# Two more steps of an attention loop turned by way of DRAM and VectorE

## The reference

```python
x = _layernorm(x + attn(x, Wq, Wk, Wv, Wg, Ws, Wo, g_norm_weight))    # 16 heads, DK 64, M 64, DV 128
x = _layernorm(x + xattn(x, ctx, xWq, bq, xWk, bk))
x = _layernorm(x + ffn(x, w_gate, w_up, w_down))
...
# attn, for each head and token t (p = exp(s - z), g the decay, z = cumlogsumexp(s)):
hk = hk * g[:, None, :] + k[..., None] * p[:, None, :];  ok = q @ hk
pv = softmax(ok)
hv = hv * g[..., None] + p[..., None] * v;               ov = pv @ hv
o  = rmsnorm(ov) * g_norm_weight * silu(x @ Wg);         y  = o @ Wo
# xattn: attention = softmax(query key^T) of ctx; x_m = x @ attention
# ffn: activations of 8 bits, ternary weights, Hadamard transform before w_down
```

## Time and profile before

| | before |
|---|---|
| median of 3 runs | 1484.67 us (1484.51 to 1484.93) |
| time of the profiled execution | 1485.11 us |
| its span, first to last instruction | 1483.3 us |
| TensorE busy | 1448.3 us (98%) |
| VectorE busy | 1091.2 us (74%) |
| ScalarE, GpSimd busy | 637.7 us (43%), 435.9 us (29%) |
| mean granted TensorE clock | 0.998 |
| DMA traffic | 166.53 MB, 112 GB/s in the mean |

### The profile page before, as it was taken

How to read it: one execution, slowest core, us unless ns; L and a number is a source line. 1 busy time by engine, 2 the same in 40 slices (tenths; PEclk the granted TensorE clock), 3 DMA queues, 4 the chain that set the end, 5 groups by cost and what they waited for, 6 DMA issues and landing times.

```text
span 1483.3 us, 23970 instructions
## 1 busy us (share of the span) xinstructions
PE 1448.3 (98%) x9240; PEld 1167.8 (79%) x9240; DVE 1091.2 (74%) x2062; ACT 637.7 (43%) x1205; POOL 435.9 (29%) x283
## 2 busy tenths in 40 slices
PE   8999999999999999999999999999999999999998
PEld 6888888888888888888888888878888646666675
DVE  5567766666667777777677687688787886977788
ACT  4333333333324333333333334234343466776775
POOL 0311011211205445435554423221421343333320
PEclk9999999999999999999999999999999999999999
DMA  4554433443524444435555311101211225444452
GB/s 158 176 138 128 120 97 104 124 119 94 152 71 136 118 139 132 132 110 130 163 157 165 118 44 51 51 8 36 78 44 35 88 79 184 122 129 144 154 172 92
DMA packets 213297, 166.53 MB, mean 112 GB/s; under 512 B 89664, under 2 KB 174528, under 8 KB 213184
## 3 DMA queue, kind: packets, MB, share of 16 engines
q1 hardware_dynamic: 191920, 133.27, 30.4%
q10 hardware_dynamic: 21264, 31.73, 7.2%
HBM read 115.02 MB, written 49.94 MB: 111 GB/s over the span
## 4 chain that ended last, share of the span: by engine, by line
PE 85%; DVE 7%; DMA 2%; POOL 2%; ACT 2%; issue 1%; SPq 0%; POOLq 0%; ACTq 0%; DVEq 0%
PE bank L490 17%; PE bank L496 17%; PE bank L493 17%; PE bank L723 6%; PE bank L618 4%; PE bank L738 4%; PE bank L759 3%; PE bank L580 2%; PE bank L553 2%; PE bank L604 2%; DVE AM L1198 1%; PE bank L575 1%; PE bank L561 1%; PE bank L588 1%; DVE OKM L1176 1%
## 5 line engine op out<-in xcount | busy, mean ns | idle before, releaser
L490 PE MATMUL bank<-Wh,X 128*128 128x512 f32 x512 | 205.6, 402 | 0.1
L496 PE MATMUL bank<-Wh,X 128*128 128x512 f32 x512 | 200.0, 391 | 0.0
L493 PE MATMUL bank<-Wl,X 128*128 128x512 f32 x512 | 199.3, 389 | 0.0
L490 PE MATMUL bank<-X,Wh 128*128 128x512 f32 x384 | 156.4, 407 | 6.3 <-ACT Wh L816 6.3
L1512 POOL TENSOR_TENSOR Wl<-RAW,Wh 128x512 fp32r<-128x512 f32 (+1 forms) x65 | 112.1, 1734 | 135.9 <-ACT Wh L816 135.8
L496 PE MATMUL bank<-X,Wl 128*128 128x512 f32 x384 | 150.8, 393 | 0.0
L493 PE MATMUL bank<-X,Wh 128*128 128x512 f32 x384 | 150.2, 391 | 0.0
L1535 POOL TENSOR_TENSOR sm<-sm,half 128x8 f32<-128x8 f32 x31 | 51.0, 1647 | 328.1 <-DVE sm L1223 328.1
L1558 POOL TENSOR_TENSOR LO<-M,HI 128x512 fp32r<-128x512 f32 x64 | 82.6, 1291 | 160.3 <-PE bank L732 128.0
L878 ACT ACTIVATE V<-bank 128x256 f32<-128x256 f32 x128 | 48.7, 381 | 182.1 <-PE bank L496 181.8
L723 PE MATMUL bank<-XT,W 128*128 128x512 bf16 x512 | 121.9, 381 | 0.6 <-DVE GS L1381 0.6
(11 more groups left out here) (223 smaller groups left out, 3280.9 us busy)
## 6 DMA issues: line engine op xcount, KB each, us to landing
z_scratch<-EV SPq DMA_DIRECT2D x64, 256.0 KB, 2.0
Z<-z_scratch SPq DMA_DIRECT2D x16, 1024.0 KB, 5.8
o_scratch<-OG ACTq DMA_DIRECT2D x96, 128.0 KB, 2.4
AM<-o_scratch ACTq DMA_DIRECT2D x24, 512.0 KB, 4.7
RAW<-wgT SPq DMA_DIRECT2D x16, 512.0 KB, 4.6
RAW<-wuT SPq DMA_DIRECT2D x16, 512.0 KB, 4.4
RAW<-wdT SPq DMA_DIRECT2D x16, 512.0 KB, 4.4
RAW<-Wo SPq DMA_DIRECT2D x14, 512.0 KB, 4.4
```

The lines of the kernel that those rows point to most:

```text
L490: engine.matmul(o, lh(c), rh(c), start=c == 0, stop=False)
L493: engine.matmul(o, lh(c), rl(c), start=False, stop=False)
L496: last = engine.matmul(o, ll(c), rh(c), start=False, stop=c == n - 1)
```

## The change

`MOVED` goes from 24 to 26. Steps 24 and 25 have K, E and OG turned by way of DRAM and VectorE; rounds 25 and 26 follow the order ALONE in place of STEP. The numbers in `PLACES` stay.

```diff
-MOVED = 24
+MOVED = 26
 
 
 def moved(n):
     return 1 < n < MOVED
```

## The result

The changed kernel takes 1487.80 us in the median of 20 runs (1484.48 to 1490.10), the kernel before, run beside it, 1485.09 (20 runs, 1483.75 to 1488.18). The ratio is 1.0013, with a 95% interval of 1.0007 to 1.0019: about 1.9 us slower (1.0 to 2.8). That is inside the 3.0 us that I called no change to be told. The forecast was +0.8: the sign is the same, the size lies just under the interval. The range, 1483.2 to 1487.6, was laid around a kernel before of 1484.67; 1.9 us on that is 1486.6, within it. The median of 1487.80 as it stands is 0.2 us above its upper end, since before too came out higher beside it, 1485.09.

What follows compares the result with a forecast made beforehand. TensorE, busy 98% of the span, was taken to bound the kernel. Terms -0.76 + 1.60 - 0.05 summed to +0.8 us, so 1485.5 us as median, with an 8-in-10 range of 1483.2 to 1487.6.

Steps and rivals of the forecast that it cites:

- K and E of step 24: Round 23 to 24: the turns fill idle VectorE time, so TensorE keeps the gain, -0.76 us.
- K and E of step 25, given back: Round 24 to 25: VectorE's turns delay its queue by 1.08 us, so TensorE's second 0.76 us is lost waiting.
- the estimate by the Trainium skill: At 311 ns per transpose, K and E would take 2.2 us on VectorE, the sum 1.1 us higher, near 1486.6.
- The stall at `turn_ok`: Round 25: TensorE, free after `sums`, waits 2.45 us for late OKM; `scores` comes 1.60 us later.
- Round 26: OG's turns save 0.85 us, but `y` waits 0.8 for a bank until VectorE makes U of `vg1`: -0.05 us.
- `y` never waits for OTl: Rival: in rounds 25 and 26 `y` waits for late OTl, giving 1487.5 to 1489.5 us; chance 0.14.
- The cover of the earlier trace: Rival: VectorE's idle time hides the turns and all 3.22 us is gained, 1481.5 us; chance 0.07.
- VectorE without gaps from the turns of round 24 to OKM: Sign expected in the changed profile: VectorE shows no gap from round 24's turns until OKM.
- Sum: Last step: -0.76 + 1.60 - 0.05 = +0.8 us, giving 1485.9 profiled and 1485.5 as median.

Runs made afterwards that it cites:

- ke2425: Kernel before with K and E of steps 24 and 25 turned by DRAM and VectorE, OG and order as before; 1485.39 us, ratio 0.9994.
- order: Kernel before with rounds 25 and 26 in the order ALONE and no further turns moved; 1487.62 us, ratio 1.0007.
- centre: Changed kernel with batch 0's centring moved from place 400 to 404, behind `turn_ok`; 1485.56 us, ratio 0.9997.
- stall: Changed kernel with batch 0's n1 moved from place 406 to 400, so normalising too stands ahead of OKM; 1492.87 us, ratio 1.0047.
- bank: Changed kernel with the hold of `vg1`'s bank for step 27 raised by one, so `y`(25) takes another bank; 1488.06 us, one run.
- sfirst: Changed kernel with `s` ahead of `turn_ok` again in rounds 25 and 26; 1485.92 us, ratio 1.0002.
- best2: `sfirst` with other places for the cross attention, centring and normalising; 1483.95 us, ratio 0.9992.
- again: The changed kernel once more, unchanged; 1487.94 us, ratio 1.0014.
- ke24: Kernel before with only K and E of step 24 turned by DRAM and VectorE, OG and order as before; 1484.97 us, ratio 0.9993.

## Why the prediction was right, and where it was short

**K and E of step 24, -0.76.** Measured -0.75 to -0.77 in every kernel that has it.

**K and E of step 25, given back.** `ke2425` gains nothing with it. L575 starts without a recorded gap; of the 0.76, 0.31 goes ahead of L561, a wait that I had named as one of two. VectorE has 1.09 us for the two turns, as the row gave it (1.08), and not the 2.2 of the estimate by the Trainium skill (VectorE: DVE Perf Modes, "The three transpose paths").

**The stall at `turn_ok`.** Predicted 2.45 us, released by OKM, measured 2.19. The time from its start to `scores` was to be 20.21 and was 20.14. A and B together gave +0.55 (-0.77 + 1.32), where I had +0.84 (-0.76 + 1.60). `order`, `centre` and `stall` show the cause as I named it, the centring ahead of OKM with only `sums` to cover it.

**Round 26.** Predicted -0.85 + 0.8 for the bank, measured -0.06 in all, with the wait at the instruction that I named; `bank` shows the two halves apart, -0.85 and +0.79.

**The rivals.** `y` never waits for OTl: OTl starts at 890.47 and ends at 891.7, where I had 893.3; the normalising took 1.9 us and not 2.98. The cover of the earlier trace rows did not hold, as the lack of gaps in the earlier trace rows said. My sign "VectorE without gaps from the turns of round 24 to OKM" was not quite met: the 0.56 us behind GpSimd stand there, and cover nothing.

**What was short.** Up to `scores` of round 26 the sum was +0.8 and the traces have +0.5 and +0.65. The runs say +1.9: that the sum came near the traces is the mechanism, that it stayed within the range of the runs owes something to the width of that range. Two terms are missing from the sum.

First, 0.35 us in the last round, far behind the change, at the wait for W in `weights` (L604): 1.6 in place of 1.2 (1.46 to 1.60 against 1.11 to 1.22). It is there in the seven traces of kernels that have K, E and OG of both steps on VectorE (the changed kernel twice, `sfirst`, `centre`, `best2`, `stall`, `bank`) and in none of the six others. The wait is for what VectorE makes from L1313 there. Why 200 us of equal work lie between, and neither part alone does it, stays open.

Second, the clock. TensorE's granted clock falls to half, 1.2 of 2.4 GHz, for 3.4 us in some executions, a few times at most. (It also falls in the last 3 to 5 us of all thirteen traces; that is not counted here.) The windows (us; busy of PE, PEld, DVE, ACT, POOL; clock; DMA) of `bank`, whose wait of 2.19 us ends at 880.27:

```profile
876.00:880.00 4.00, 2.09 (x32) 1.72 (x30) 3.69 (x13) 1.91 (x4) 2.07 (x4) 1.00 0.49 141
880.00:884.00 4.00, 3.73 (x12) 3.15 (x13) 2.09 (x5) 0.63 (x1) 2.58 (x3) 0.57 0.44 150
884.00:890.00 6.00, 6.00 (x30) 4.95 (x29) 3.12 (x6) 2.85 (x6) 1.28 (x1) 1.00 0.28 95
```

and of the changed kernel, where the same wait at the same time was followed by full clock:

```profile
876.00:880.00 4.00, 1.84 (x30) 1.51 (x28) 3.73 (x13) 1.73 (x4) 2.30 (x5) 1.00 0.50 149
880.00:884.00 4.00, 3.96 (x20) 3.34 (x21) 2.36 (x5) 0.63 (x1) 2.37 (x2) 1.00 0.49 139
```

In the same 4 us the one shows 12 matmuls at a clock of 0.57 and the other 20 at 1.00, and B is 67.07 - 65.52 = 1.55 us longer. In `stall` the clock falls within the wait of 5.96 us, at 882.5, and stays low for 6.8 us, 4.5 of them work behind the wait, which lengthened B by the further 2.1:

```profile
880.00:886.00 6.00, 1.18 (x5) 1.18 (x6) 5.21 (x10) 0.00 (x0) 3.40 (x3) 0.71 0.53 168
886.00:892.00 6.00, 6.00 (x20) 4.74 (x20) 2.98 (x4) 1.53 (x3) 0.00 (x0) 0.72 0.13 50
```

Of the four traces with a wait of 2 us or more at `turn_ok` two have such a fall (`bank`, `stall`), of the nine others none.

That this reaches the runs is seen in their clocks. A fall of 3.4 us at half the clock takes about 0.0011 off the mean clock of a span of 1484 us, and the traces bear it out: those with no fall but the one at the end have 0.999 or 1.0, those with one 0.998, with two 0.997, `bank` with three 0.996, `stall` with a double one and two more 0.995. So a run's clock counts its falls. Over the 32 runs of the changed kernel (20 and 12) the mean clock is 0.9974, over the 76 of before beside the experiments 0.9980 (on the chip of `again` alone 0.9974 and 0.9981, where I expected a difference of 0.0003 or more). `stall`, with the wait made longer, has 0.9956, as expected below that of the changed kernel; `centre`, with the wait gone, has 0.9985, as expected not below before. A clock of 0.996 or less stands in 12 of the 38 runs of the kernels with a wait of 2 us or more at `turn_ok`, and in none of the 154 runs of the others. The mean clock alone says less: `ke2425` and `ke24`, without that wait, have 0.9976 and 0.9977, before on their chip 0.9978.

In before, runs at 0.997 take 1486.9 us in the mean and those at 0.999 1484.6, so 0.0006 of clock are about 0.6 us. At equal clock the changed kernel is slower by 1.4 (at 0.997), 1.7 (0.998) and 0.9 us (0.999). So of the 2.0 us between the means of these runs an estimated 0.6 go with the clock, 0.9 are waits that the traces show (+0.5 and +0.35), and about 0.5 is not placed; the clocks are read to 0.001 only, which is 1 us, and the two sets were not all run side by side. That a wait of this length makes a fall behind it more frequent is what `stall`, `centre` and these counts show; why it comes in some executions and not in others is not shown. The step of the prediction that falls short is its last one, "Sum": each wait was priced by its own length alone.

## What to carry to other kernels

Work taken from the engine that sets the pace is won only where the queue of the engine that gets it has a gap right there: VectorE's free fifth of the round was no help, its rows without gaps ahead of OKM were the thing to read. When a change comes with another order, price the order by itself first; here it cost 1.3 us in the trace with nothing moved, and with `s` ahead of `turn_ok` and the cross attention's places fitted to it the same move of turns gains 2.9 us in the trace. And a new wait of 2 us in a dense stretch can cost more than 2 us, by the clock behind it, so look at the clock of many runs and not of one.

## What the runs showed of the hardware that was not expected

The clock falls at much the same few places, in a part of the executions: at 1224.6 in before, between 1182 and 1238 in eight other traces, and behind the wait of 2.08 us for the mask in round 27, which every trace has. TensorE there in `ke24`, where the fall came, and in before, where it did not:

```profile
992.06 3.37 PE L622 MATMUL bank<-V,AM 128*128 128x128 f32 x16 [2.08 <-DVE AM L1202]
```

```profile
992.75 2.05 PE L618 MATMUL bank<-V,AM 128*128 128x128 f32 x16 [2.08 <-DVE AM L1198]
```

The same 16 matmuls after the same wait take 3.37 us in the one and 2.05 in the other. Five of thirteen traces have the fall there, and D is 193.28 to 193.56 in these and 192.28 to 192.62 in the others. The windows of before show its own fall, later:

```profile
1218.00:1224.00 6.00, 4.46 (x20) 1.87 (x17) 5.75 (x12) 5.62 (x12) 1.79 (x2) 1.00 0.15 57
1224.00:1229.00 5.00, 4.23 (x17) 2.79 (x17) 2.71 (x7) 4.15 (x8) 1.26 (x1) 0.66 0.23 89
```

One fall costs 1.0 to 1.3 us by D and 1.55 by B of `bank`, where the expectation of `ke24` had 1.6 for any, against the 1.9 us of this change, and by the clocks above the number of falls makes a good part of the 4 us over which one kernel's runs spread.

The turn of 128x1024 takes 1.23 us on VectorE, less than twice the 0.66 of 128x512, and TensorE's own turns cost 0.11 us each in a row: `bank` gets back 0.85 us for 8 of them, so that what VectorE takes for OG is longer than what TensorE is rid of.
